# Softmax row sums from keys added beforehand on VectorE, and a first GRU tile whose last rows are turned from where they lie

## What is computed

```
xn   = rms_norm(x, g_norm) * (1 + scale) + shift          # scale, shift = cond @ W_emb + b_emb
q, k, v = heads(xn @ W_qkv)                               # 16 heads of 32; q and k normed per head
o    = softmax(q k^T / sqrt(32)) v
x1   = x + o + o @ W_out
# GRU over the 256 rows of each sequence, first state cond
r, z = sigmoid(x1_t @ W_ih + h @ W_hh, ...); n = tanh(i_n + r * h_n)
h    = (1 - z) * n + z * h
out  = x1 + h
```

## Time and profile before

| what | value |
|---|---|
| median of three runs | 1704.15 us (1703.97 to 1704.56) |
| profiled execution: its time / its span | 1703.24 us / 1701.2 us |
| TensorE busy in the span | 1665.6 us (98%) |
| VectorE / ScalarE / GpSimd busy | 1104.8 / 830.7 / 469.2 us |
| granted TensorE clock, mean | 0.99 |
| row sums (L612), busy, 1024 records | 69.6 us |
| products with V (L605), busy, 1024 records | 70.3 us |
| maxima (L890) on VectorE, 128 instructions | 150.4 us |
| attention stage, up to the first GRU input product | 693.73 us |

### The profile page before, as it was taken

The page is one execution under the profiler, slowest core; times in us unless marked ns, Lnnn a source line. Parts: engine busy times, 40 slices in busy tenths (PEclk is TensorE's granted clock), DMA queues, the critical chain, the costliest instruction groups (busy, mean ns, idle before and its releaser), DMA issues.

```text
span 1701.2 us, 70109 instructions
## 1 busy us (share of the span) xinstructions
PE 1665.6 (98%) x30293; PEld 1163.0 (68%) x30293; DVE 1104.8 (65%) x4016; ACT 830.7 (49%) x2267; POOL 469.2 (28%) x531
## 2 busy tenths in 40 slices
PE   8899999999999998899999999999999999999998
PEld 6566666666666664577777777777777777777775
DVE  5666667667766754466666666666666666666665
ACT  4655655566656552344444444444444444444443
POOL 4555555555555530111111111111111111111111
PEclk9999999999999998999999999999999999999999
DMA  6223433333343327311111111111111111111110
GB/s 199 81 76 96 96 90 88 92 90 94 93 101 92 90 76 159 95 25 31 27 29 30 27 29 29 27 31 28 28 31 27 28 31 27 29 29 27 31 25 15
DMA packets 233229, 99.92 MB, mean 59 GB/s; under 512 B 141180, under 2 KB 213704, under 8 KB 232920
## 3 DMA queue, kind: packets, MB, share of 16 engines
q1 hardware_dynamic: 232800, 95.40, 22.3%
q10 hardware_dynamic: 120, 0.04, 0.0%
HBM read 58.38 MB, written 36.96 MB: 56 GB/s over the span
## 4 chain that ended last, share of the span: by engine, by line
PE 96%; DVE 1%; ACT 1%; issue 1%; DMA 1%; POOL 0%; SPq 0%; DVEq 0%; ACTq 0%; POOLq 0%
PE ps L789 39%; PE ps L660 20%; PE ps L516 16%; PE ps L625 5%; PE ps L605 4%; PE ps L588 3%; PE ps L612 3%; PE ps L565 2%; PE ps L583 2%; PE ps L572 1%; DMA wstage<-in_L_cond_W_qkv_dram 1%; PE ps L552 1%; PE ps L537 0%; DVE wql L876 0%; DVE nmx L890 0%
## 5 line engine op out<-in xcount | busy, mean ns | idle before, releaser
L660 PE MATMUL ps<-wih,x1T 128*32 128x192 f32 x8192 | 379.2, 327 | 1.2 <-ACT ps L1357 1.2
L1502 POOL TENSOR_TENSOR outG<-hG,x1g 128x128 f32<-128x128 f32 x255 | 116.5, 457 | 889.5 <-DVE hG L1067 889.5
L789 PE MATMUL ps<-whh,hTE 128*32 128x192 f32 x8192 | 355.0, 326 | 1.1 <-DVE hTE L1074 1.1
L789 PE MATMUL ps<-whh,hTO 128*32 128x192 f32 x8192 | 355.0, 326 | 0.0
L1370 ACT ACTIVATE v<-ps 128x128 f32<-128x128 f32 x512 | 140.5, 274 | 413.2 <-PE ps L789 413.2
L660 PEld LDWEIGHTS ps<-wih,x1T 128*32 128x32 f32 x8192 | 246.7, 110 | 89.6 <-ACT ps L1357 1.6
L789 PEld LDWEIGHTS ps<-whh,hTE 128*32 128x32 f32 x8192 | 232.2, 109 | 101.9 <-DVE hTE L1074 21.8
L789 PEld LDWEIGHTS ps<-whh,hTO 128*32 128x32 f32 x8192 | 232.2, 110 | 100.6 <-DVE hTO L1074 20.3
L1047 DVE SCALAR_TENSOR_TENSOR v<-v,ps 128x64 f32<-128x64 f32 x512 | 113.4, 221 | 248.2 <-ACT v L1370 248.2
L890 DVE TENSOR_REDUCE nmx<-ps 128x4 f32<-128x1024 f32 x128 | 150.4, 1217 | 135.3 <-PE ps L565 135.3
L1378 ACT ACTIVATE v<-v 128x64 f32<-128x64 f32 x512 | 131.4, 257 | 133.0 <-DVE v L1052 133.0
(11 more groups left out here) (149 smaller groups left out, 1999.7 us busy)
## 6 DMA issues: line engine op xcount, KB each, us to landing
xres<-in_x_dram SPq DMA_DIRECT2D x32, 256.0 KB, 3.0
xscr<-x1s SPq DMA_DIRECT2D x32, 256.0 KB, 2.1
xblk<-x1s SPq DMA_DIRECT2D x128, 64.0 KB, 2.7
x1g<-xscr SPq DMA_DIRECT2D x128, 64.0 KB, 2.0
out_dram<-outG SPq DMA_DIRECT2D x252, 32.0 KB, 1.7
x1n<-xblk SPq DMA_DIRECT2D x124, 64.0 KB, 1.8
kscr<-kx SPq DMA_DIRECT2D x30, 256.0 KB, 2.0
kx<-kscr SPq DMA_DIRECT2D x60, 128.0 KB, 2.6
```

Source lines behind the costliest of these rows:

```text
L660: last = pe.matmul(gb[pr % 2][q][32 * j:32 * j + 32, 64:256], x1T[:, tt % 2, r, c, :], wig[:, c, :, 128 * j + 64 * q:128 * j + 64 * q + 64 ...
L789: last = pe.matmul(gb[e][q][32 * j:32 * j + 32, 0:192], h[:, c, :], whg[:, c, :, 128 * j + 64 * q:128 * j + 64 * q + 64], start=False, sto ...
L1502: g_.tensor_tensor(outG[:, tt % 2, k, :], hG[:, t % 2, :], x1g[tt % 2][:, k // 2, :], ALU.add).then_inc(s_og, 1)
```

## The change

1. `row_sums(G)` makes one product per head instead of two: its operand is a new buffer `PS`, the sum of the two key tiles of PT. It waits for a new semaphore, `p_sums`.
2. VectorE makes `PS` in `add_tiles(G, h)`, two instructions per group of two heads each (128 x 512 float32, both inputs in SBUF). They stand in the loop of group G - 1, after its last work, and wait for the exponentials of G and for the row sums of G - 1, which have read `PS`.
3. For w = 0, `turn_x` moves ahead of `squares(n, 1, 0)`, and `normalize(n, 1, 1)` moves behind the adds.
4. `out_sum(14, 1)` moves ahead of the maxima of group 62.
5. The DMA of ScalarE into `x1n0` is gone. `x1n0` is cleared by GpSimd beforehand; TensorE turns it before the last output chunk, and four small products then turn the eight rows of sequence 15 straight from `x1s` into every sixteenth column of the same bank. ScalarE writes the seeds before it copies the tile out.
6. The two turns of the first state move ahead of `out_sum(15, 0)` on VectorE.

```diff
             def row_sums(G):
 
-                for k in range(2):
-                    for j in range(4):
-                        last = pe.matmul(pR[32 * j:32 * j + 32, :], ones, PT[:, G % 2, k, j, :], start=(k == 0), stop=(k == 1))
+                pe.wait_ge(s_ps, 2 * G + 2)
+                for j in range(4):
+                    last = pe.matmul(pR[32 * j:32 * j + 32, :], ones, PS[:, j, :], start=True, stop=True)
                 last.then_inc(s_pv, 1)
...
+            def add_tiles(G, h):
+
+                j = slice(2 * h, 2 * h + 2)
+                v.wait_ge(s_ex, 2 * G + h + 1)
+                if G:
+                    v.wait_ge(s_pv, G)
+                v.tensor_tensor(PS[:, j, :], PT[:, G % 2, 0, j, :], PT[:, G % 2, 1, j, :], ALU.add).then_inc(s_ps, 1)
...
+                if w == 1 and n == NB:
+                    out_sum(b - 1, 1)
                 if G + 1 < NP:
                     maxima(G + 1, 0)
                     maxima(G + 1, 1)
...
                     if G == 0:
                         x_sums(2)
-                    squares(n, 1, 0)
-                    normalize(n, 1, 1)
-                    if G == 0:
-                        x_mean(2)
                     elif m < NB:
                         turn_x(m)
+                    squares(n, 1, 0)
...
+                if G + 1 < NP:
+                    add_tiles(G + 1, 0)
+                    add_tiles(G + 1, 1)
+                if w == 0 and n < NB:
+                    normalize(n, 1, 1)
...
             def turn_first_x1(bank):
                 v = bank.rearrange("p (c t) -> p c t", c=KC)
-                pe.wait_ge(s_xf, 16 * (ST + 1))
+                pe.wait_ge(s_xf, 16 * ST)
...
+            def turn_last_rows(bank):
+
+                v = bank.rearrange("p (c t) -> p c t", c=KC)
+                emptied(pe, ("out", NB - 1, 0))
+                for c in range(KC):
+                    last = pe.transpose(v[:, c, NB - 1::NB], x1s[0][0:ST, 128 * c:128 * c + 128], ident[0:ST, 0:ST])
                 last.then_inc(s_1T, 1)
...
+            turn_first_x1(ps[:, 5, :])
             for i in range(2):
                 out_chunk(i, KC - 1)
-            turn_first_x1(ps[:, 5, :])
+            turn_last_rows(ps[:, 5, :])
```

More of the change, by code:

```diff
@@ L171, in cond_resid_kernel @@
         a_P = base[0]
+        PS = sb("PS", [128, 4, T])
         kx = sb("kx", [128, 2, D])
@@ L239, in cond_resid_kernel @@
             sem(n) for n in ("projected", "squared", "reduced", "rsqrt", "normed", "turned", "v_kept"))
-        s_S1, s_mx, s_nT, s_S, s_ex, s_pv, s_rt, s_ri, s_rb, s_o, s_oh, s_ol, s_op = (
-            sem(n) for n in ("rounded_scores", "maxima", "maxima_turned", "scores", "exps", "pv", "sums_turned", "recips",
+        s_S1, s_mx, s_nT, s_S, s_ex, s_ps, s_pv, s_rt, s_ri, s_rb, s_o, s_oh, s_ol, s_op = (
+            sem(n) for n in ("rounded_scores", "maxima", "maxima_turned", "scores", "exps", "p_sums", "pv", "sums_turned", "recips",
                              "recips_turned", "o", "o_high", "o_low", "out_proj"))
@@ L351, in load_x1 @@
                 for k in range(ST):
+                    if k == 0:
+                        sp.wait_ge(s_hz, 4)
                     sp.dma_start(x1n0[NB * k:NB * k + NB - 1, :], xscr[k, 0:NB - 1, :]).then_inc(s_xf, 16)
@@ L643, in turn_first_x1 @@
                 v = bank.rearrange("p (c t) -> p c t", c=KC)
-                pe.wait_ge(s_xf, 16 * (ST + 1))
+                pe.wait_ge(s_xf, 16 * ST)
                 for c in range(KC):
-                    last = pe.transpose(v[:, c, :], x1n[0][:, 128 * c:128 * c + 128], ident)
+                    pe.transpose(v[:, c, :], x1n[0][:, 128 * c:128 * c + 128], ident)
+            def turn_last_rows(bank):
[3 more added lines that the diff above has]
+                    last = pe.transpose(v[:, c, NB - 1::NB], x1s[0][0:ST, 128 * c:128 * c + 128], ident[0:ST, 0:ST])
                 last.then_inc(s_1T, 1)
@@ L981, in _ @@
             squares(1, 0, 1)
+            add_tiles(0, 0)
+            add_tiles(0, 1)
             for G in range(NP):
@@ L1006, in _ @@
                         x_sums(2)
-                    squares(n, 1, 0)
-                    normalize(n, 1, 1)
-                    if G == 0:
-                        x_mean(2)
                     elif m < NB:
                         turn_x(m)
+                    squares(n, 1, 0)
+                elif w == 0:
+                    out_sum(b - 1, 0)
                 elif w == 1 and n < NB:
@@ L1024, in _ @@
                     squares(m, 0, 1)
[L1025 to L1028, removed]
+                if G + 1 < NP:
[3 more added lines that the diff above has]
+                    normalize(n, 1, 1)
+                    if G == 0:
+                        x_mean(2)
                 if G in (1, 2):
@@ L1031, in _ @@
                     wo_low(2 * G - 1)
-            out_sum(NB - 1, 0)
             v.wait_ge(s_b0, 64)
@@ L1037, in _ @@
             v.transpose(hs, window(0)).then_inc(s_hs, 1)
+            out_sum(NB - 1, 0)
             out_sum(NB - 1, 1)
@@ L1349, in _ @@
             high(NP - 1)
-            emptied(s, ("out", NB - 1, 0))
-            s.dma_start(x1n0[NB - 1:128:NB, :], x1s[0][0:ST, :]).then_inc(s_xf, 16)
-            keep_first_x1(ps[:, 5, :])
             def seed(pr):
@@ L1363, in _ @@
             seed(1)
+            keep_first_x1(ps[:, 5, :])
             for t in range(T):
@@ L1488, in _ @@
                     g_.wait_ge(s_qkv, 6 * NB)
-                    for h in (hG, hTE, hTO):
+                    for h in (hG, hTE, hTO, x1n0):
                         g_.memset(h, 0.0).then_inc(s_hz, 1)
```

## The result

The changed kernel takes 1691.23 us (median of six, 1689.66 to 1698.33) beside 1703.06 us of the kernel before: a ratio of 0.9936, 95% interval 0.9919 to 0.9954. It is faster, but by 12 us where I had said 22, and it lies 0.2 us above the upper end of my range. The profiled execution took 1691.07 us, its span is 1689.2 us.

What follows compares the result with a forecast made beforehand. TensorE was taken to bound the steady attention stage: 25.4 us of row sums less 6.4 us of waits, plus 3.5 us at the tail, gave 22.5 us off and 1681.6 us. Range 1675 to 1691 us.

Steps and rivals of the forecast that it cites:

- What bounds the kernel, and what leaves TensorE: Steady attention stage: TensorE is full; half the row sums leave it, 0.43 us per group, 59 groups, 25.4 us.
- The price of an add: VectorE's two 128x512 adds per group: 0.60 us from start to start, 0.69 us long, 0.98 us at most.
- w = 0: First group of a sequence: adds at 302.43 to 303.63 use idle VectorE time; key norm 0.6 us later, nothing lost.
- w = 1, the weak place: Adds behind `turn_k` wait for late keys; row sums wait 1.0 us in some 6 of 15 sequences; 6.4 us in all.
- The maxima in w = 1, "0.3 us to spare": VectorE's maxima end at 306.56, their turn on TensorE comes at 306.88; 0.3 us to spare, nothing lost.
- The tail: End of attention stage: a wait for `wih`, 41.4 us after `whh`, replaces removed waits; gain 3.5 us, 2.8 to 3.9.
- The GRU "as before": GRU stage behind the attention stage: keeps its loop as it is, nothing counted there.
- The wait becomes the rule: Keys land late in all 15 sequences: waits of 15.3 us instead of 6.4, 1690.5 us; chance 0.12.
- GpSimd holds up the adds: At w = 0 GpSimd's `rq` keeps adds out 0.6 us, waits of w = 2 grow, 9 us: 1690.6 us; chance 0.06.

Runs made afterwards that it cites:

- without adds: Changed kernel with the adds and their semaphore removed and row sums made from the first key tile alone: 1677.44 us, ratio 0.9854.
- the adds ahead of the norm: Changed kernel with VectorE's two adds of w = 1 moved ahead of `normalize(n, 0, 0)`, still behind `turn_k`: 1677.88 us, ratio 0.9865.
- the later `wo_low`: Changed kernel with two `wo_low` pairs moved from groups 1 and 2 to 3 and 4: 1689.55 us; with the adds ahead of the norm too, 1678.31 us.
- short adds in w = 3: Changed kernel whose two adds in w = 3 add only 16 of 256 columns per head: 1683.56 us, ratio 0.9896.

## Why the prediction was wrong, step by step

- *What bounds the kernel, and what leaves TensorE.* Right in kind: TensorE is full from 100 us on, and without adds a sequence gets 1.55 us shorter, of the 1.72 that I had counted. I counted 59 groups; the first eight gave 0.9 us instead of 3.0 even without adds, and a ScalarE copy in w = 1 took 0.17 us per sequence.
- *The price of an add.* **This step failed.** "0.60 us step / 0.69 long" held wherever `rq` was the neighbour, and 0.98 us "bounds one add from above" did not hold: 1.21 us (1.82 less the first add's 0.61). It was not even the slowest row of that shape in the trace of before. The first key norm of w = 0 took 1.99 us there, and 1.99 to 2.34 in 13 sequences, while GpSimd ran an instruction of 1.90 us (it writes `xb`). And the 0.98 us row had `low` beside it. Timelines of VectorE and GpSimd before the change:

```profile
297.15 1.99 DVE L846 TENSOR_TENSOR kx<-kx,rq 128x512 f32<-128x512 f32 x1
```

```profile
296.70 1.90 POOL L1411 TENSOR_TENSOR xb<-xb,rxp 128x1024 f32<-128x1024 f32 x1
...
306.75 0.74 POOL L1435 TENSOR_TENSOR ol<-oS,oh 128x256 fp32r<-128x256 f32 x1
```

In both the VectorE instruction ends 0.54 us after GpSimd's (299.14 and 298.60; 308.03 and 307.49), as the add in the changed kernel does. So what an add can cost was to be read before the change: it waits for the end of the GpSimd instruction and then takes 0.54 to 0.55 us. I used a row as a bound without asking what stretched it, and then put the adds in a place where `low` comes.
- *w = 0.* Right: adds at 301.04 and 301.90, the key norm 0.69 us idle, nothing lost.
- *w = 1, the weak place.* Right place, wrong cause; **the sum for this wait failed with the price of the add.** I had moved the keys 0.6 us later, but left GpSimd's `rq` at 311.9, where it was before; in the changed kernel it comes 0.56 us later, since an add of w = 3 holds up an `msq`. That moved the adds by 0.6 us, and `low` held up the second by 0.53 more. Together that is 1.1 us, and the row sums come 1.08 us later. Keys that land late were to hold up `turn_k` in six sequences; in fact GpSimd's chain and `low` held up the adds in all fourteen. 6.4 us of waits were 12.7, and they cost 15 (14 x 1.08; the first input product comes 15.0 us later in the changed kernel than in the one without adds).
- *The maxima in w = 1, "0.3 us to spare".* Held; no row of the changed kernel waits for them in the steady part.
- *The tail.* Right: the wait for `wih` took the place of the removed ones, the first input product came 41.16 us after `whh` for 41.4, and 4.3 us came for 3.5.
- *The GRU "as before".* Its loop is. But the first products are not: 2.81 us for 64, where it was 4.92. The granted clock says why:

```profile
670.00:680.00 10.00, 5.67 (x36) 3.48 (x37) 3.53 (x8) 3.15 (x6) 2.35 (x3) 0.80 0.32 71
684.00:690.00 6.00, 5.90 (x148) 5.73 (x152) 0.88 (x5) 1.10 (x5) 0.00 (x0) 1.00 0.58 124
```

In the changed kernel they run at 2.4 GHz. With the adds ahead of the norm the first 64 took 4.35 us, from 669.35. The windows of that kernel:

```profile
660.00:670.00 10.00, 4.84 (x24) 3.55 (x27) 2.01 (x4) 1.29 (x3) 0.00 (x0) 0.50 0.70 219
669.00:676.00 7.00, 6.65 (x128) 5.10 (x132) 0.27 (x2) 0.55 (x3) 0.00 (x0) 0.75 0.61 142
```

TensorE, which had stood 7.23 us for `x1n`, was at 1.2 GHz up to the first product and for some 3 us more (a mean of 0.75 over 7 us is half the time at 0.50), then at 2.4. My prediction put this term at nothing; it gave 2.4 us, by luck. In the profiled executions that differ in this the GRU stage differs by 1 to 3 us (the changed kernel, and the two with the later `wo_low`: 1004.9 to 1005.4; the other kernels of the experiments 1006.4 to 1008.0).
- *The rivals.* "The wait becomes the rule" gave the right time, 1690.5, from the wrong cause. "GpSimd holds up the adds" had the right cause in the wrong place: I looked only at w = 0 and at `rq`, which did no harm (300.34 to 303.24, with two adds of 0.68 and 0.69 us beside it), and not at `low` and `msq`. The Trainium skill, SBUF — State Buffer, section "SBUF: two separate sides", says that of a VectorE instruction with two SBUF inputs and a GpSimd instruction that reads SBUF the first to start holds the other off for its whole instruction. For `low`, `msq` and the adds the traces agree (second add 0.06 us late: +0.53 us; `msq` 0.08 us late: +0.47 us; short adds in w = 3: the order turns and `low` pays). For a VectorE instruction that starts while `rq` runs they don't, as the earlier trace rows had shown; the other way round, an `rq` that starts behind a norm, 3.21 us for 2.90 speaks for it in part. I had let one instruction speak for all of GpSimd's.

## What to carry to other kernels

Before moving work to an engine, list what runs on its neighbour at that place in every phase of the loop, and take from the trace the duration of the same shape beside each of those instructions, not the commonest one; a stretched row is a question, not a bound. Sort all rows of that shape by their length before you call one the slowest. Work that only waits for data already there belongs ahead of an instruction that waits for another engine: two lines moved were worth 13 us here, more than the change itself had brought. A gain on the bounding engine is cut off where another engine's list was just in time, so count the spare time at every handover, not only at the one that looks weak.

## What the runs showed of the hardware

- VectorE's adds and norms (128x512, 0.69 us) and GpSimd's `low`, `msq` and `xb` ran one behind the other when they met. An add or norm that started second ended 0.54 to 0.55 us after GpSimd's instruction (0.98, 1.22 and 1.99 us long), and 0.05 us between the two starts was enough to settle the order. GpSimd's 2.90 us `rq` (128x16) did not stretch a VectorE instruction that started beside it; started 0.22 us behind a norm, it took 3.21 us itself.
- Eight small loads issued behind a 1.5 MB one landed 4.1 us after their last issue instead of 1.5; the large one landed 6.5 us after its issue began, for 6.2 to 6.7 us behind them.
- The same first 64 products of the GRU took 2.81 us or 4.21 to 5.35 us in the kernels with the new end. They took 2.81 in the three in which TensorE had stood 2.9 to 3.0 us for `x1n`, and 4.21 to 5.35 in those in which it had stood 3.7 to 7.2. Within the latter the longest standing did not give the longest time (7.24 us: 4.21; 4.09 us for `x1n` and 4.60 for `wih`: 5.35). That it is the standing was read from the traces and not tried by itself.
